# Scan layer: half of the weighing on GpSimd, diagonals on ScalarE, skip term on TensorE

## What is computed

```python
xz = layernorm(x) @ w_in;  x_b, z = split(xz)          # 256 inner channels each
x_b = silu(causal_conv(x_b))
B_mat, C_mat = split(x_b @ w_xproj)                    # 16 states each, per token
dt = softplus(x_b @ w_dt + b_dt);  A = -exp(A_log)     # A: 256 x 16
def step(h, ins):                                      # over the 512 tokens
    dt_t, B_t, C_t, x_t = ins
    h = exp(dt_t[:, :, None] * A) * h + dt_t[:, :, None] * B_t[:, None, :] * x_t[:, :, None]
    return h, einsum('bdn,bn->bd', h, C_t)
y = scan(step, 0, ...) + D * x_b
out = (y * silu(z)) @ w_out + residual
```

## Time and profile before

| | us |
|---|---|
| Median of 3 runs (1726.14 to 1727.53) | 1726.68 |
| Profiled execution, its own time | 1724.85 |
| Profiled execution, its span | 1723.1 |
| Busy in the span: PE | 1400.1 |
| DVE | 1218.5 |
| ACT | 729.0 |
| POOL | 706.2 |

### The profile page before, as it was taken

The page is one execution under the profiler, slowest core; times in us unless marked ns, Lnnn a source line. Parts: engine busy times, 40 slices in busy tenths (PEclk is TensorE's granted clock), DMA queues, the critical chain, the costliest instruction groups (busy, mean ns, idle before and its releaser), DMA issues. The chain is left out here.

```text
span 1723.1 us, 26589 instructions
## 1 busy us (share of the span) xinstructions
PE 1400.1 (81%) x9106; PEld 942.8 (55%) x9106; DVE 1218.5 (71%) x2920; ACT 729.0 (42%) x1224; POOL 706.2 (41%) x905
## 2 busy tenths in 40 slices
PE   4799999939996549977588899889996387489998
PEld 3333333326874328853466566667884177367786
DVE  5777777374555675556799899678777744669776
ACT  2276767621214112136544343355554411154554
POOL 3824241027622137600366566036664051006665
PEclk9599999969998769989799999899998699689999
DMA  1144230000100001100000000444440000065443
GB/s 41 61 126 131 79 137 2 1 25 25 34 16 12 25 0 38 37 18 1 0 1 1 1 1 1 180 118 117 136 132 17 0 1 1 1 216 129 134 133 105
DMA packets 73239, 96.21 MB, mean 56 GB/s; under 512 B 24656, under 2 KB 42592, under 8 KB 72608
## 3 DMA queue, kind: packets, MB, share of 16 engines
q1 hardware_dynamic: 73120, 94.71, 18.9%
HBM read 84.42 MB, written 10.26 MB: 55 GB/s over the span
## 5 line engine op out<-in xcount | busy, mean ns | idle before, releaser
L526 DVE CUSTOM_DVE_ANT_1 la_neg<-bank,la_table 128x512 f32<-128x512 f32 x256 | 166.3, 688 | 44.8 <-PE bank L617 44.2
L1656 POOL TENSOR_TENSOR lh_h_low<-lh_hidden,lh_h_high 128x512 fp32r<-128x512 f32 x84 | 111.4, 1328 | 161.5 <-ACT lh_h_high L1689 161.2
L1454 PEld LDWEIGHTS bank<-le_diag,le_dtxT 128*128 128x128 f32 x1024 | 126.5, 191 | 80.5 <-issue 59.0
L1454 PE MATMUL bank<-le_diag,le_dtxT 128*128 128x128 f32 x1024 | 142.0, 282 | 25.4 <-DVE le_h L1372 21.3
L1372 DVE TENSOR_TENSOR_SCAN le_h<-le_keep,bank 128x512 f32<-128x512 f32 x128 | 155.2, 1213 | 3.8 <-PE bank L1454 3.8
L1656 POOL TENSOR_TENSOR lf_h_low<-lf_hidden,lf_h_high 128x512 fp32r<-128x512 f32 x84 | 111.5, 1329 | 109.1 <-ACT lf_h_high L1689 108.8
L1310 ACT ACTIVATE le_keep<-le_dt,le_A 128x512 f32<-128x512 f32 x128 | 92.1, 722 | 133.1 <-DVE le_h L1372 133.1
L453 ACT ACTIVATE la_probT<-bank 128x512 f32<-128x512 f32 x256 | 135.6, 605 | 12.9 <-PE bank L636 10.9
L1225 POOL TENSOR_TENSOR le_hc<-le_hc 128x512 f32<-128x512 f32 x64 | 81.0, 1266 | 101.4 <-DVE le_hc L1381 97.6
L1679 ACT ACTIVATE bank<-bank 128x512 f32<-128x512 f32 x144 | 83.7, 581 | 62.0 <-PE bank L1844 60.3
L1233 POOL TENSOR_TENSOR le_diag<-ident,le_bT 128x512 f32<-128x512 f32 x64 | 71.3, 1136 | 71.3 <-ACT le_bT L1297 70.3
(11 more groups left out here) (568 smaller groups left out, 3534.3 us busy)
## 6 DMA issues: line engine op xcount, KB each, us to landing
lf_weight<-lf_scratch SPq DMA_DIRECT2D x128, 128.0 KB, 3.0
lh_weight<-lh_scratch SPq DMA_DIRECT2D x128, 128.0 KB, 3.0
la_table<-la_scratch SPq DMA_DIRECT2D x4, 1792.0 KB, 7.3
lf_weight<-lf_scratch SPq DMA_DIRECT2D x64, 64.0 KB, 2.2
lh_weight<-lh_scratch SPq DMA_DIRECT2D x64, 64.0 KB, 2.2
la_bias_parts<-la_scratch_parts SPq DMA_DIRECT2D x12, 248.0 KB, 6.3
lb_w1s<-in_L_ffn_w_dram SPq DMA_DIRECT2D x8, 256.0 KB, 2.8
lb_w2s<-in_L_ffn_w_dram SPq DMA_DIRECT2D x8, 256.0 KB, 3.1
```

The costliest lines, as they stand in the source:

```text
L526: dve.tensor_tensor_reduce(out=neg[:, u % 2, :].rearrange("p (c i) -> p c i", i=P), in0=k.bank[u % RING1][:].rearrange("p (c i) -> p c i", ...
L1454: last = pe.matmul(k.bank[4 + q % 2][:, j * P:(j + 1) * P], dtxT[:, (g * G2 + bb) * TPB + j, c, :], diag[:, d % DIAGS, j, :], start=True, ...
L1656: pool.tensor_tensor(h_low[:, u % RING, :], hidden[:, u % RING, :], h_high[:, u % RING, :].bitcast(F32), ALU.subtract)\
```

## The change

Within the scan layer alone:

- VectorE weighs only the even unit of each pair; its order becomes scan, scan, weigh. GpSimd weighs the odd one itself and then adds the two. It cannot read the banks, so the odd C rows reach it through memory: SP stores the C rows once to a scratch tensor, and then loads one row per block, repeated over 128 partitions (256 KB), into a ring of three.
- ScalarE builds the diagonals, four 128x128 activations each with the B column as scale, two diagonals per block after the first. They stand in its stream behind `keep` for units 1 and 2 of a block, and wait for the pushes that still read the slot.
- The skip term's D moves into two diagonals `skip`, which ScalarE builds once; `open_sums` uses them in place of the identity, and VectorE's multiplication before the loop goes.
- TensorE spreads one C row per block, a block ahead. Before the transposes it issues 22 idle products, once the first half of the logarithm is done.
- The output product of a sequence waits only for the gates of that sequence.

```diff
-    LAG, GATE_AT, PAIRS, DIAGS = 3, 3, 3, 4
+    LAG, GATE_AT, PAIRS, DIAGS, ROWS = 3, 3, 3, 4, 3
+    BLOCKS = UNITS // (2 * C)
...
+        c_row = sb("c_row", [P, ROWS, T])
+        skip = sb("skip", [P, C, P])
+        scratch = nc.dram_tensor(f"{tag}_scratch", [N, B * T], F32)
...
+            sp.wait_ge(rows_ready, B)
+            sp.dma_start(scratch[:, :], rows_b[N:2 * N, :, :].rearrange("n b t -> n (b t)")).then_inc(rows_stored, 16)
+            sp.wait_ge(rows_stored, 16)
+            for blk in range(BLOCKS):
+                g, bb, _, n = unit(blk * 2 * C + 1)
+                if blk >= ROWS:
+                    sp.wait_ge(pool_weighed, (blk - ROWS + 1) * C)
+                row = bass.AP(scratch, n * B * T + (g * G2 + bb) * T, [[0, P], [1, T]])
+                sp.dma_start(c_row[:, blk % ROWS, :], row).then_inc(row_loaded[blk % ROWS], 16)
 
...
-            def pair_up(p):
-                pool.wait_ge(hc_ready, 2 * p + 2)
+            for p in range(UNITS // 2):
+                blk = p // C
+                pool.wait_ge(row_loaded[blk % ROWS], 16 * (blk // ROWS + 1))
+                pool.wait_ge(scanned, 2 * p + 2)
+                if p >= PAIRS:
+                    pool.wait_ge(paired, p - PAIRS + 1)
+                pool.tensor_tensor(hc[:, p % PAIRS, 1, :], h[:, (2 * p + 1) % UN, :], c_row[:, blk % ROWS, :], ALU.mult).then_inc(pool_weighed, 1)
+                pool.wait_ge(pool_weighed, p + 1)
+                pool.wait_ge(weighed, p + 1)
                 pool.tensor_tensor(hc[:, p % PAIRS, 0, :], hc[:, p % PAIRS, 0, :], hc[:, p % PAIRS, 1, :], ALU.add).then_inc(paired, 1)
...
-            def build(d):
-                g, bb, _, n = unit(d // 2 * 2 * C + d % 2)
-                if d >= DIAGS:
-                    pool.wait_ge(pushed, (d // 2 - 1) * 2 * C)
-                b = g * G2 + bb
-                column = bT[:, b * TPB:(b + 1) * TPB, n].unsqueeze(2).to_broadcast([P, TPB, P])
-                pool.tensor_tensor(diag[:, d % DIAGS, :, :], bcast(k.ident[:, 0:1], (0, TPB), (1, P)), column, ALU.mult).then_inc(diag_ready, 1)
-
-            pool.wait_ge(bT_ready, 1)
-            for d in range(DIAGS):
-                build(d)
-            for blk in range(UNITS // (2 * C)):
-                pair_up(2 * blk)
-                for d in (2 * blk + DIAGS, 2 * blk + DIAGS + 1):
-                    if d < UNITS // C:
-                        build(d)
-                pair_up(2 * blk + 1)
...
             act.activation(bT[:], k.bank[4][:].rearrange("p (t n) -> p t n", n=2 * N)[:, :, 0:N], ACT.Copy).then_inc(bT_ready, 1)
+
+            def build(d):
+                g, bb, _, n = unit(d // 2 * 2 * C + d % 2)
+                if d >= DIAGS:
+                    act.wait_ge(pushed, (d // 2 - 1) * 2 * C)
+                b = g * G2 + bb
+                for j in range(TPB):
+                    last = act.activation(diag[:, d % DIAGS, j, :], k.ident[:], ACT.Copy, scale=bT[:, b * TPB + j, n:n + 1])
+                last.then_inc(diag_ready, 1)
+
+            for c in range(C):
+                act.activation(skip[:, c, :], k.ident[:], ACT.Copy, scale=cols[:, 2, c:c + 1]).then_inc(skip_ready, 1)
+            act.wait_ge(bT_ready, 1)
+            for d in range(DIAGS):
+                build(d)
...
                 if q >= UN:
                     act.wait_ge(scanned, q - UN + 1)
                 act.activation(keep[:, q % UN, :], dt_[:, c, g * G2 + bb, :], ACT.Exp, scale=A[:, c, n:n + 1]).then_inc(keep_ready, 1)
+                d = q // (2 * C) * 2 + 2 + (q % (2 * C) - 1)
+                if q >= 2 * C and q % (2 * C) in (1, 2) and d < UNITS // C:
+                    build(d)
...
-            dve.wait_ge(bT_done, 1)
-            dve.wait_ge(dtx_ready, C)
-            for c in range(C):
-                dve.tensor_scalar(xc[:, c, :, :], xc[:, c, :, :], cols[:, 2, c:c + 1], None, ALU.mult).then_inc(skip_ready, 1)
...
                 dve.wait_ge(keep_ready, q + 1)
                 dve.wait_ge(pushed, q + 1)
                 if q >= UN:
-                    dve.wait_ge(hc_ready, q - UN + 1)
+                    dve.wait_ge(pool_weighed if q % 2 else weighed, (q - UN) // 2 + 1)
                 dve.tensor_tensor_scan(h[:, i, :], keep[:, i, :], k.bank[4 + q % 2][:], 0.0, ALU.mult, ALU.add).then_inc(scanned, 1)
 
-            def weigh(q):
-                _, _, _, n = unit(q)
-                p = q // 2
-                dve.wait_ge(scanned, q + 1)
-                dve.wait_ge(c_done, q // (2 * C) * 2 + n % 2 + 1)
+            def weigh(p):
+                blk = p // C
+                dve.wait_ge(scanned, 2 * p + 1)
+                dve.wait_ge(c_done, blk + 1)
                 if p >= PAIRS:
-                    dve.wait_ge(paired if n % 2 else summed, p - PAIRS + 1)
-                dve.tensor_tensor(hc[:, p % PAIRS, n % 2, :], h[:, q % UN, :], k.bank[6 + n % 2][:], ALU.mult).then_inc(hc_ready, 1)
+                    dve.wait_ge(summed, p - PAIRS + 1)
+                dve.tensor_tensor(hc[:, p % PAIRS, 0, :], h[:, 2 * p % UN, :], k.bank[6 + blk % 2][:], ALU.mult).then_inc(weighed, 1)
...
@@ -1390,9 +1406,8 @@
                 scan(q)
                 if q % Q == GATE_AT and q > Q:
                     gate(q // Q - 1)
-                if q:
-                    weigh(q - 1)
-            weigh(UNITS - 1)
+                if q % 2:
+                    weigh(q // 2)
...
             pe.wait_ge(gated, C * B)
+            pe.wait_ge(soft_ready, 1)
+            k.idle_products(pe, 22, 7)
             pe.wait_ge(dtx_ready, C)
             pe.wait_ge(bT_ready, 1)
...
-            def spread_c(d):
-                g, bb, _, n = unit(d // 2 * 2 * C + d % 2)
-                if d >= 2:
-                    pe.wait_ge(hc_ready, (d // 2 - 1) * 2 * C + 2 * C - 2 + n % 2 + 1)
-                pe.matmul(k.bank[6 + n % 2][:], spread[:, n, :], bc[:, g * G2 + bb, :], start=True, stop=True).then_inc(c_done, 1)
+            def spread_c(blk):
+                g, bb, _, n = unit(blk * 2 * C)
+                if blk >= 2:
+                    pe.wait_ge(weighed, (blk - 1) * C)
+                pe.matmul(k.bank[6 + blk % 2][:], spread[:, n, :], bc[:, g * G2 + bb, :], start=True, stop=True).then_inc(c_done, 1)
...
                 for i in range(UN):
-                    pe.matmul(k.bank[i][:], k.ident[:], xc[:, i % C, g * G2 + i // C, :], start=True, stop=False, skip_group_check=True)
+                    pe.matmul(k.bank[i][:], skip[:, i % C, :], xc[:, i % C, g * G2 + i // C, :], start=True, stop=False, skip_group_check=True)
...
-                if q >= 2 * C and q % (2 * C) < 2:
-                    spread_c(q // (2 * C) * 2 + q % (2 * C))
+                if q >= 2 * C and q % (2 * C) == 0 and q // (2 * C) + 1 < BLOCKS:
+                    spread_c(q // (2 * C) + 1)
                 accumulate_at(q)
             for step in range(UNITS, UNITS + LAG):
                 accumulate_at(step)
-            pe.wait_ge(gated, C * B + C * B)
             for g in range(B):
+                pe.wait_ge(gated, C * B + (g + 1) * C)
```

More of the change, by code:

```diff
@@ L1197, in layer_scan @@
         rows_ready, rest_ready, mid_ready = sem("rows_ready"), sem("rest_ready"), sem("mid_ready")
-        scanned, hc_ready, summed, gated = sem("scanned"), sem("hc_ready"), sem("summed"), sem("gated")
+        scanned, weighed, pool_weighed, summed, gated = sem("scanned"), sem("weighed"), sem("pool_weighed"), sem("summed"), sem("gated")
+        rows_stored, row_loaded = sem("rows_stored"), [sem(f"row_loaded{i}") for i in range(ROWS)]
         out_done, added, x_ready = sem("out_done"), sem("added"), sem("x_ready")
```

## The result

The changed kernel took **1698.1 us** (median of 4 runs, 1696.8 to 1699.3) against 1726.4 (median of 4, beside it): a ratio of 0.983, 95% interval 0.981 to 0.985. The forecast was 1694, range 1683 to 1709. Its profiled execution took 1697.44 us with a span of 1695.7.

What follows compares the result with a forecast made beforehand. VectorE sets the pace, with TensorE close behind. Loop -24.9, ahead of the loop -4.1 and end -3.6 sum to -32.6 us, taking 1726.7 to 1694; range 1683 to 1709.

Steps and rivals of the forecast that it cites:

- The loop's chain: In the loop, scan 4k, push, spread, accumulate, push, scan 4k+3 makes VectorE wait 0.60 us; a block takes 6.28.
- The first block: At the loop's start, open_sums stands between pushes 2 and 3, so scan 4 comes 8.64 us after scan 0.
- The last three scans: At the loop's end, scan 127 comes 4.35 us into the last block, which has no spread.
- The change of group: Mid-loop, the gate and TensorE's lower clock behind it add 8.1 us to the loop; about 1.7 less with clock kept.
- The gate's part: At the change of group, the gate puts scan 68 at 9.26 us in place of 6.28: +2.98.
- The other part: At the change of group, scan 71 comes 9.68 us after scan 68 in place of 4.57: +5.11.
- Ahead of the loop: Before the first scan, shorter VectorE operations and faster transposes save 4.1 us, ends 1.6 and 5.
- The contention term: Ahead of the loop, without GpSimd's builds VectorE's last two additions and products each take 2.29 us: -1.57.
- The transposes' term: Ahead of the loop, idle products warm TensorE's clock, so 32 transposes take 3.9 us: -2.5, or 0 if it doesn't hold.
- The end: From the last scan to the end of the last addition: 13.65 us in place of 17.25, -3.6.
- the forecast's term for the residual pieces: In four blocks with sixteen 0.48 us pieces, ScalarE is over by up to 1.7 each: 0 to 7 us, taken as 0.
- Row transfers: In the loop, C rows land in 3.1 us, issued two blocks (12 us) ahead, and cost nothing.

Runs made afterwards that it cites:

- The two experiments on order: Two separate edits of the changed kernel: accumulates issued behind odd pushes (1676.9 us), and the spread issued behind push 4k+3 instead of ahead of it (1690.8 us).
- the third: Changed kernel with only one of each diagonal's four 128-column parts built on ScalarE in the loop: 1698.8 us.
- both edits: Changed kernel with accumulates behind odd pushes, plus 34 idle products ahead of the transposes and 9 ahead of the last accumulate: 1674.7 us.

## Why the prediction held, point by point

- **The loop's chain.** Right in each link (0.15, 0.96, 0.22, 0.86, 1.15 against 0.15, 0.97, 0.22, 0.86, 1.16) and in its sum, 6.27 against 6.28. Scan 4k+3 comes 0.61 late (906.79 against 905.05 + 1.13), forecast 0.60; the profile counts 0.52 of it as idle. The two experiments on order show that it is the cause, and the third that the builds are not.
- **The first block** 8.64 (843.10 to 851.74), as forecast. The last three scans 4.33 against 4.35.
- **Two blocks of 30** took 6.63, with a wait of 0.87 at one scan in place of 0.52. Blocks like them stand in several of the kernels here. The profile names no releaser, and the cause stays open; together they cost 0.7.
- **The change of group.** The gate's part was right: the scan behind it came at 955.35, 9.25 after scan 64, forecast 9.26. The other part, 9.68 to scan 71, was 10.74 (955.35 to 966.09): 1.1 too little. I had taken the slow push and sums as before; after the change TensorE waited 3.50 in place of 3.30, and at the lower clock the push took 2.05 in place of 1.50 and open_sums 5.48 in place of 4.95. How much of them the lower clock takes differs between executions: with idle products at head and end and the same loop, scan 71 came 9.68 after scan 68, the forecast to the hundredth, and with the spread or the builds changed 10.8 and 11.0. So the 1.1 is not a fixed size, and the 9.68 there is luck.
- **Ahead of the loop.** The contention term was right: both VectorE operations took 2.28 and 2.29 when nothing ran on GpSimd, and the transposes became ready 1.6 earlier within the layer. The transposes' term, -2.5, was the largest miss: they went from 6.38 to 5.38, -1.0. The step that failed was that the idle products would end as the transposes became ready. They ended 2.85 us before, because the clock rose part-way through them (0.50 up to 829.2, 1.00 behind it) and 22 took 6.31, not 9.6; then it fell again, and the transposes ran at 0.59 of full speed for the first 4 us. The prediction had named 0 for a clock that does not hold; the 1.0 lies between that and its 2.5.
- **The end.** 14.62 in place of 13.65. The handovers were smaller than the 0.15 taken, but the accumulate after a wait of 2.09 us ran at 1.2 GHz, and the output product came 1.87 after it and not 0.86.
- **ScalarE.** A build took 0.387, against 0.40 taken and 0.479 as the upper end. Neither its start nor its waits cost the loop anything that shows: the list of waits has 1.1 us in two waits for `keep` in the whole loop, one of them (0.60) at the change of group, ahead of the wait of 6.02 for the push, the other the usual 0.52 of a block. Where the chain is gone the forecast's term for the residual pieces shows, small: with the accumulate behind odd pushes one scan, in a block that holds four of them, waits 0.6 us for `keep`.
- **GpSimd.** 1.273 for the multiplication, against 1.27 taken. The rule on engine selection of the Trainium skill ("GPSIMD Engine Reference", section 4.1), which speaks against the change, holds for the price and not for the time. The multiplication is 1.9 times VectorE's 0.66, and the kernel gained because it lay beside the path. With one more operation a pair it did not lie there, and the kernel was slower than before, 1740.
- **Row transfers.** None released anything.

Together the three clock terms are 1.1 + 1.5 + 1.0 = 3.6 us, and the two long blocks 0.7; the blocks' last hundredth gives 0.4 back. That is 3.9, where the layer's -28.8 and the forecast's -32.6 lie 3.8 apart.

## What to carry to other kernels

When the engine that sets the pace is relieved, find its next wait before counting the gain: write the instruction order of the engine behind it between two of its steps. Here TensorE was not full, yet its written order (an accumulate between two pushes) gave back 0.6 us a block of the 1.4 that VectorE had saved (7.08 to 5.64), and moving one product by one step returned it. A releaser in a list of waits is the last to report, and taking its work away is the test.

## What the runs showed that I had not expected

TensorE's clock fell behind short waits. It was still at 2.4 GHz in the 2.85 us between idle products and transposes and at the start of the transposes (1.00 from 832.65 to 836.0), and at 1.2 GHz right behind that (0.50 from 836.1 to 839.4). It was at 1.2 GHz behind a wait of 2.09 us at the end (0.98 from 1055.9 to 1058, 0.50 from 1058 to 1060). Once it had risen while idle products ran, 22 of them took 6.31 us, so a count of idle products that is right at the lower clock leaves a gap at the higher one: 34 covered it.

Behind one and the same wait it fell in one execution and not in another. These are the push and open_sums at the change of group, with the accumulate behind odd pushes alone (first two rows) and with both edits (last two):

```profile
942.42 2.05 PE L1471 MATMUL bank<-le_diag,le_dtxT 128*128 128x128 f32 x8 [2.90 <-DVE le_h L1389]
944.26 4.38 PE L1494 MATMUL bank<-le_xc,le_skip 128*128 128x512 f32 x8
...
942.42 1.13 PE L1471 MATMUL bank<-le_diag,le_dtxT 128*128 128x128 f32 x8 [2.90 <-DVE le_h L1389]
943.39 3.60 PE L1494 MATMUL bank<-le_xc,le_skip 128*128 128x512 f32 x8
```

From 942.5 to 945.8 the granted clock is 0.50 in the first and 1.00 in the second, after the same 2.90 us of waiting. The difference is 1.7 us, as much as the prediction put on the clock there.
